# Output projections of a windowed attention in halves, and one scaling moved ahead of a sum, in a two-layer transformer kernel

## The reference, cut to what matters

```python
def _layer(x, ...):                     # x: 2 x 1024 x 128
    h = shift_token(x)                  # second half of the features, one token back
    q, k, v = jnp.split(h @ wqkv, 3)    # 8 heads of 64
    q, k = rotary_xpos(l2norm(q) * qs, l2norm(k) * ksc)
    o = local_attention(q, k, v)        # windows of 64, own window and the one before
    x = x + o @ wo                      # 512 -> 128
    h = shift_token(x)
    h = layernorm(h) * lg + lb
    a, g = jnp.split(h @ w1 + b1, 2)    # 341 each
    return x + (a * gelu(g)) @ w2 + b2
for l in range(2):
    x = _layer(x, ...)
```

## Time and profile before

| what | value |
|---|---|
| median of 3 runs | 562.44 us (561.64 to 563.48) |
| the profiled execution | 562.2 us |
| its span in the profile | 560.4 us |
| busy share: TensorE, VectorE, ScalarE, GpSimd | 87%, 77%, 62%, 60% |
| chain that ended last, by engine | TensorE 63%, VectorE 19%, GpSimd 9%, no visible wait 4%, ScalarE 3%, DMA 1% |
| granted TensorE clock | 90% or more of full speed in 37 of 40 slices, in all from the seventh on |

### The profile page before, as it was taken

The page is one execution under the profiler, slowest core; times in us unless marked ns, Lnnn a source line. Parts: engine busy times, 40 slices in busy tenths (PEclk is TensorE's granted clock), DMA queues, the critical chain, the costliest instruction groups (busy, mean ns, idle before and its releaser), DMA issues.

```text
span 560.4 us, 11701 instructions
## 1 busy us (share of the span) xinstructions
PE 485.5 (87%) x4017; PEld 306.7 (55%) x4017; DVE 432.2 (77%) x1172; ACT 348.7 (62%) x1002; POOL 334.7 (60%) x259
## 2 busy tenths in 40 slices
PE   5541037999999999999989999999999999999997
PEld 3311014467777766543457777776544445767775
DVE  6899999889999875656899999985455688466665
ACT  4961004689999997543579999997647526533332
POOL 5850006999999998476899999994010267420000
PEclk9995569999999999999999999999999999999999
DMA  8400002311111112000031111111000000000000
GB/s 284 168 0 1 1 2 78 71 33 41 39 39 39 34 36 85 2 1 1 1 113 40 40 39 36 35 39 34 5 3 0 0 1 1 1 0 20 20 20 20
DMA packets 14880, 19.93 MB, mean 36 GB/s; under 512 B 2362, under 2 KB 8996, under 8 KB 14692
## 3 DMA queue, kind: packets, MB, share of 16 engines
q1 hardware_dynamic: 14532, 19.08, 12.5%
q10 hardware_dynamic: 288, 0.08, 0.1%
HBM read 8.94 MB, written 1.05 MB: 18 GB/s over the span
## 4 chain that ended last, share of the span: by engine, by line
PE 63%; DVE 19%; POOL 9%; issue 4%; ACT 3%; DMA 1%; SPq 0%; DVEq 0%; POOLq 0%; ACTq 0%
PE psT L1394 9%; PE psQK L1467 8%; PE psO L1589 5%; PE psQK L1603 5%; PE psQK L1783 5%; PE psO L1521 5%; PE psS L1569 4%; DVE vst L990 3%; DVE vAB L994 3%; PE psO L1394 3%; POOL rn L819 3%; PE psS L1855 3%; PE psO L1855 2%; PE psQK L1715 2%; PE psS L1692 2%
## 5 line engine op out<-in xcount | busy, mean ns | idle before, releaser
L526 ACT ACTIVATE prob<-psS,nmx 128x128 f32<-128x128 f32 x256 | 90.1, 377 | 17.4 <-DVE nmx L1135 17.4
L819 POOL TENSOR_TENSOR rn<-ssq,half 128x16 f32<-128x16 f32 x32 | 93.1, 2909 | 6.9 <-DVE ssq L1121 6.7
L811 POOL TENSOR_TENSOR ra<-ra,rb 128x512 f32<-128x512 f32 x64 | 80.6, 1278 | 1.0 <-DVE rb L1103 0.8
L666 POOL TENSOR_TENSOR rst<-mv,half 128x4 f32<-128x4 f32 x24 | 25.7, 1071 | 78.6 <-DVE mv L922 66.6
L1467 PE MATMUL psQK<-wqkv,hsA 128*128 128x512 f32 x128 | 61.2, 596 | 0.9 <-DVE hsA L1084 0.6
L526 ACT ACTIVATION_READ_ACCUMULATOR prob<-psS,nmx 128x1 f32 x256 | 55.3, 216 | 0.0
L1100 DVE TENSOR_TENSOR ra<-psQK,rope 128x512 f32<-128x512 f32 x64 | 43.9, 685 | 9.5 <-PE psQK L1467 9.1
L827 POOL TENSOR_TENSOR qkn<-ra,rn 128x512 f32<-128x512 f32 x32 | 49.6, 1549 | 2.5
L1135 DVE TENSOR_REDUCE nmx<-psS 128x4 f32<-128x512 f32 x64 | 41.0, 683 | 4.5 <-PE psS L1569 4.5
L1103 DVE TENSOR_TENSOR rb<-psQK,rope 128x512 f32<-128x512 f32 x64 | 43.5, 680 | 0.0
L647 ACT ACTIVATE gel<-psQK 128x512 f32<-128x512 f32 x32 | 19.1, 598 | 37.5 <-PE psQK L1783 37.5
(11 more groups left out here) (238 smaller groups left out, 1182.8 us busy)
## 6 DMA issues: line engine op xcount, KB each, us to landing
vAB<-vAB SPq DMA_DIRECT2D x62, 128.0 KB, 2.2
wqkv<-in_wqkv SPq DMA_DIRECT2D x2, 768.0 KB, 7.6
big<-in_x SPq DMA_DIRECT2D x4, 256.0 KB, 5.3
ropeb<-in_rope SPq DMA_DIRECT2D x1, 1024.0 KB, 5.7
big<-in_ew SPq DMA_DIRECT2D x2, 512.0 KB, 4.0
wmod<-in_wmod SPq DMA_DIRECT2D x2, 384.0 KB, 6.1
out<-big SPq DMA_DIRECT2D x3, 256.0 KB, 2.3
w<-in_w SPq DMA_DIRECT2D x2, 341.0 KB
```

Of the source, the lines that this page charges most:

```text
L526: act.activation(prob[:, k, :], psS[:, hb, c * P:(c + 1) * P], ACT.Exp, bias=nmx[:, k:k + 1], accum_out=sums[:, n % 2, k:k + 1]).then_inc( ...
L811: pool.tensor_tensor(o, o, rb[:, r], ALU.add).then_inc(s["sum_" + name], 1)
L819: pool.tensor_tensor(rn[:, :], ssq[:, :], half[:, :], ALU.pow).then_inc(s["rn_ready"], 1)
```

## The change

`out_proj` is split into `out_low` (two products that open the sum in psQK and leave it open) and `out_high` (the other two, which close it and count `wo_done`). TensorE's rounds 13 to 15 are laid out anew with these halves, `turn(l, 0)` moves from the head of round 14 to behind its weighing, and VectorE's `mid` and `ln` move accordingly: tile 13 is scaled ahead of `mid` of group 0, `ln` of group 0 stands behind the scaling of tile 14, `mid` of group 1 ahead of the scaling of tile 15. Both layers get it. The MLP's use of `out_proj` for group 3 is unchanged.

```diff
--- before.py
+++ after.py
@@ -1204,17 +1204,19 @@
                     rope_products(n + 3, 0)
                 if has(i + 2) and i > 2 - LEAD:
                     q_normed(n + 2)
-                if i == NT - 2:
-                    ln(ln_no(2 + l, 0))
                 if has(i + 1) and i > 2 - LEAD:
                     negmax(n + 1, 0)
                     negmax(n + 1, 1)
+                if i == NT - 1:
+                    mid(l, 1)
+                if has(i):
+                    o_scaled(n)
                 if i == NT - 3:
                     mid(l, 0)
-                if has(i):
-                    o_scaled(n)
-                if i >= NT - 2:
-                    mid(l, i - NT + 3)
+                if i == NT - 2:
+                    ln(ln_no(2 + l, 0))
+                if i == NT - 1:
+                    mid(l, 2)
                 if has(i + 3) and i > -LEAD:
                     sum_squares(n + 3, 1)
                     sum_squares(n + 3, 0)
@@ -1596,12 +1598,20 @@
                 pe.wait_ge(s["o_norm"], n + 1)
                 four(psO[:, 0, :], lambda k: osb[:, k * P:(k + 1) * P]).then_inc(s["oT_fill"], 1)
 
-            def out_proj(l, g):
+            def out_low(l, g):
                 if g:
                     pe.wait_ge(s["zmid"], l * NG + g)
-                for c in range(4):
-                    i = mm(psQK[:, 0, :], wo[:, c, :], oT[:, c, gsl(g)], start=(c == 0), stop=(c == 3))
+                for c in range(2):
+                    mm(psQK[:, 0, :], wo[:, c, :], oT[:, c, gsl(g)], start=(c == 0), stop=False)
+
+            def out_high(l, g):
+                for c in range(2, 4):
+                    i = mm(psQK[:, 0, :], wo[:, c, :], oT[:, c, gsl(g)], start=False, stop=(c == 3))
                 i.then_inc(s["wo_done"], 1)
+
+            def out_proj(l, g):
+                out_low(l, g)
+                out_high(l, g)
 
             def turn(l, g):
 
@@ -1618,13 +1628,11 @@
                     pe.wait_ge(s["ld_wl"], 16 * 4 * (l + 1))
                     pe.wait_ge(s["rope_q"], 2 * NT * (l + 1))
                     pe.wait_ge(s["sq_q"], NT * (l + 1))
-                    out_proj(l, 0)
-                if i == NT - 2:
-                    pe.wait_ge(s["rope_k"], 2 * NT * (l + 1))
-                    pe.wait_ge(s["sq_k"], NT * (l + 1))
-                    turn(l, 0)
+                    out_low(l, 0)
                 if has(i):
                     turn_p(l, i)
+                if i == NT - 1:
+                    out_high(l, 1)
                 if has(i + 1):
                     scores(l, i + 1)
                 if has(i):
@@ -1646,12 +1654,19 @@
                         pe.wait_ge(s["kT_evac"], 1)
                         keep_clock(8, psT1[:, :])
                     turn_qk(l, i + 2)
+                if i == NT - 2:
+                    pe.wait_ge(s["rope_k"], 2 * NT * (l + 1))
+                    pe.wait_ge(s["sq_k"], NT * (l + 1))
+                    turn(l, 0)
+                    out_low(l, 1)
                 if i == NT - 1:
+                    out_low(l, 2)
                     ln_t2(ln_no(2 + l, 0))
-                if i >= NT - 2:
-                    out_proj(l, i - NT + 3)
+                    out_high(l, 2)
                 if has(i):
                     turn_o(l, i)
+                if i == NT - 3:
+                    out_high(l, 0)
 
             def late_t1(kind, g):
                 if kind == 0:
```

## The result

The changed kernel takes 558.34 us (median of 4 runs, 558.07 to 558.89), the kernel before 562.04 beside it (561.60 to 563.48): a ratio of 0.993 (95% interval 0.9917 to 0.9943). The forecast was 558.2 us, faster, within 557.2 to 560.8. A second time, later and with six runs, it took 557.81 against 562.63, 0.9916 (0.9903 to 0.9929).

The account below looks back on a forecast made before the run. TensorE, busy most of the span, was taken to bound the kernel, its pauses before the MLP costing time. 1.01 + 0.95 + 0.31 less 0.16 is 2.12 us a layer, twice 4.2: from 562.44 to 558.2 us, range 557.2 to 560.8.

Parts of the forecast that it names:

- The 1.01, the 0.95 and the 0.31 us: TensorE's pauses before turning tile 13's output, weighing tile 15 and turning lnx; all claimed to go, in each layer.
- Every cover named for a wait: Work laid before each wait in the new order, such as 0.2 us spare at tile 14's probabilities, 2.4 at lnx.
- The joints: Edges between TensorE's projection halves and other work: 0.1 us behind a weighing, nothing for turnings behind projections.
- The third rival: Sums left open cost TensorE up to 0.59 us at each of twelve edges: 565.3 us; slower from 0.35 an edge; chance 0.04.
- The last wait: TensorE before the MLP, waiting for ScalarE's copy of the last output: 0.41 us claimed to become 0.57.
- The port: First layer: GpSimd and VectorE share a port pair; group 0's second copy taken as 0.42 us, ending at 218.1.
- the 1.12 us operation: GpSimd's phase-table operation, 216.27 to 217.39 in the first layer; claimed to hold group 0's first copy until some 217.7.
- The L921 that the choice rested on: Small VectorE operation, 0.17 us at 219.33 amid GpSimd's 3.65 us operation; taken to show VectorE gets through at times.
- The sum: Per layer 1.01 + 0.95 + 0.31 gained, 0.16 given back: 2.12 us; twice that is 4.2 us.
- The first: Rival: first layer, GpSimd's 3.65 us operation holds group 0's second copy to 221.4; 1.9 us left, 560.5; chance 0.2.
- The second: Rival: group 1's copies held by GpSimd, or 0.2 us spare before tile 14's turning missing; 559.2 us; chance 0.12.
- The fourth: Rival: the pauses only change place, an unseen wait taking what is gained; 562.4 us; chance 0.04.

Follow-up runs that it names:

- the probe with three more copies: Changed kernel with three more 64x512 VectorE copies behind the two for group 0; one execution only, stretches 26.18 and 24.52 us against 24.02 and 23.94.
- rounds 14 and 15 alone: Kernel before with only groups 1 and 2 in halves, group 1's sum ahead of tile 15's scaling; 559.69 us against 562.37, ratio 0.9952.
- round 13 alone: Kernel before with only group 0's part: halves, tile 13 scaled first, hsM's turning and statistics moved; 560.18 us against 562.37, ratio 0.9956.
- the held run: Changed kernel with GpSimd's 3.65 us operation replaced by two ordinary sums, so the LRU's numbers differ; 560.21 us against 562.51, ratio 0.9970.
- the scaling moved alone: Kernel before with only tile 13's scaling put ahead of group 0's sum on VectorE; 562.62 us against 562.37, ratio 1.0001.

## Why the prediction was right, point by point

**The pauses.** The 1.01, the 0.95 and the 0.31 us went, in both layers, as laid out, and the two runs with half of the change put 1.1 on round 13 and 1.0 on the rest. Every cover named for a wait held, but for 0.08 us at the turning of tile 15's probabilities (below).

**The joints.** Halves take 1.72 us (206.66 to 208.38). An edge costs 0.1 us where the half stands before a weighing (222.49 to 224.31 is 1.82), which was not counted, and as much behind one (225.39 to 227.21), which was. Before transposes it costs nothing. The third rival, 0.35 us an edge, is refuted.

**The last wait.** It was to grow from 0.41 to 0.57; it is 0.44. ScalarE's copy of the last output started at 230.05, and its table load had ended at 229.92: the small first use behind the load costs it 0.1, not 0.2, and hn came a little sooner. Together with 0.05 less for the turning of hsM this makes up for the uncounted edge: 24.04 forecast, 23.94 measured in the second layer.

**The port.** The step that could have undone it came out on the right side, for a reason that the prediction had only in part, and partly by luck. It had the first copy meet the 1.12 us operation and end near 217.7, and the second run free. In fact GpSimd was 0.3 us earlier against the stretch (216.52 is 9.86 behind its start, before 217.47 was 10.16), so that the first copy met the 3.65 us operation's own beginning and took 1.28 us; the second ran free in its middle. The 0.42 us were laid out for a copy that begins only 0.2 us behind the start of the 3.65 us operation, and there the runs show a copy held: by the first copy's end, 1.32 us behind that start, the second would have ended near 218.8 and not at 218.1 (an estimate from these rows). The L921 that the choice rested on stood 1.86 us behind the start, in the part that the probe with three more copies shows to be free.

Why GpSimd was earlier, the prediction missed: holding goes both ways. Before, VectorE's two copies ran from 214.97 to 215.85, over GpSimd's small operations ahead of the 1.12 us one; moved away, they leave them alone. GpSimd before, then changed:

```profile
214.87 0.57 POOL L736 TENSOR_SCALAR fr<-fr 128x1 f32<-128x1 f32 x2
215.52 0.64 POOL L738 TENSOR_TENSOR fr<-fr 128x1 f32<-128x1 f32 x2
```

```profile
214.21 0.46 POOL L736 TENSOR_SCALAR fr<-fr 128x1 f32<-128x1 f32 x2
214.75 0.46 POOL L738 TENSOR_TENSOR fr<-fr 128x1 f32<-128x1 f32 x2
```

That is 0.11 and 0.18 us, together the 0.29. The two runs of half the change bear it out: rounds 14 and 15 alone, with the copies where they were, has 0.57 and 0.64 and the 3.65 us operation 10.17 behind the start; round 13 alone has 0.46 twice and 9.86.

 So VectorE was some 0.4 us later for negmax of tile 15 (218.32, 11.66 behind the start; laid out 11.29), and TensorE lost 0.08 of it (221.54 to 222.49 is 0.95, where the second layer has 0.87). That is the whole difference between the layers, 24.02 and 23.94. The Trainium skill, page SBUF — State Buffer, section Who interferes with whom, has whichever of the two issues first, here GpSimd, hold the shared pair of ports for the whole instruction. For GpSimd's sums the runs agree (copies of 2.14 and 2.46 us under them). For the 3.65 us operation they don't: the copy at 217.86 took 0.43. The held run shows about what the rule would have made of the change had it applied.

**The sum.** 4.2 us were forecast, 4.36 are in the two stretches; 3.7 us in the medians of the first comparison and 4.8 in the second stand around it. Two things that lie outside the stretches differ between the profiles: the clock's fall between the layers (0.9 us), and the time at which the first stretch starts, from 206.66 to 207.98 us over the fourteen of them. That the scatter of the medians comes of these is likely, not shown: the two programs that were profiled twice started within 0.15 us of themselves.

**The rivals.** The first was refuted by the trace. Its price of 2.3 us agrees with the 2.9 of the held run, in which the turning of hsM starts 0.57 us later against the stretch (221.37 - 206.71 = 14.66 for 14.09). The second named the right suspects (group 1's copies took 0.95 and 1.23 us under GpSimd); the scaling was done at 228.3 and TensorE needed it at 229.36, so a microsecond was to spare. The fourth, pauses that only change place, is what the scaling moved alone does, but not the change.

## What to carry to other kernels

A wait at the end of a pipeline can be filled by cutting work that has slack into pieces of the wait's size, and each piece must also free what stands behind it: moving VectorE's part alone gained nothing, moving it with the halves of group 0 and the turning of hsM 1.1 us a layer. Lay the new order end to end with pitches from the old trace and check each wait against it; here that came out within 0.1 us of 24. Before moving a VectorE copy, look at what GpSimd runs at the new place and at the old one. At the new place the copy may last to some 0.3 us behind the end of GpSimd's operation (so under its sums and the 1.12 us operation; under the 3.65 us one only near its start and its end); at the old place GpSimd's operations can get shorter, and what it runs afterwards comes earlier.

## What the runs showed of the hardware that was not expected

- GpSimd's tensor_scalar with two additions over 128x1024 takes 3.65 us, where the one with a product and a sum takes 1.12, and it does not hold VectorE's copies throughout: a copy begun 0.04 us after its start took 1.28 us, three begun 1.3 to 2.3 us after it took 0.42 or 0.43, one begun 2.7 after was held to the end. What in the operation makes the free part, no run shows.
- VectorE's copies hold GpSimd as well: two pairs of its 128x1 operations take 0.57 and 0.64 us under two copies of 64x512, 0.46 and 0.46 without.
- The same program with the same pause of 1.88 us on TensorE shows a granted clock of 1.00 behind it in one execution and of 0.50, the 1.2 GHz level, in another.
